# The last feed-forward in sixteen units, with batch 0 carried through the end of the causal attention

## Chip, core and metric

The kernel is one program on one core of a Trainium2 chip. The metric is the device time of one execution in microseconds (us). The time of the kernel before is 565.87 us, the median of three runs from 564.69 to 566.86 us.

## What is computed

The input x holds 2 batches of 256 tokens with 128 features. Four pairs of an attention and a feed-forward are added to it in turn. Only the last feed-forward block matters here; cut to its second half, it is

```
x = x + einsum(attn, wo)                      # causal self-attention, 16 heads of 8
h = x * rsqrt(mean(x*x) + eps) * ln2_w        # per token
p = softmax(h @ gate_w.T)                     # 8 experts
top 2 of p, divided by their sum -> wfull[token, expert], 0 elsewhere
out = 0
for e in range(8):                            # FFN = 256
    g = silu(h @ w1[e].T) * (h @ w3[e].T)
    out = out + (g @ w2[e].T) * wfull[:, e]
x + out
```

All experts are computed for all tokens, in float32, and weighted afterwards.

## The kernel before

The 512 tokens are four tiles of 128 tokens; tiles 0 and 1 are batch 0, tiles 2 and 3 are batch 1. Each engine has one instruction list, written out by hand, and the engines meet only in counting semaphores; `wait_ge(s.name, n)` holds the engine's whole list until the count is there. No planner reorders anything, so the order in the text is the order on the engine.

The causal attention is `attention(2)` on TensorE (PE), ScalarE (ACT) and VectorE (DVE). It runs over 8 groups of 4 heads (`G = 8`); groups 0 to 3 are batch 0, groups 4 to 7 are batch 1. It is a software pipeline of 12 steps: at step s PE does the maxima of group s (`scores_max`), the scores of group s - 2 (`scores_exp`, read by ACT's Exp at L603), probabilities times values of group s - 3 (`probs_values`, L1731 and L1734) and turns the output of group s - 4 (`turn_out`, L1754), after ACT has copied it out (L620); DVE then divides it by its denominators into `Onat` (L944, L947) and counts `o_ready`. From step 8 on no maxima are left: steps 8 to 11 are the drain.

After it come, for all four tiles at once and one behind the other: `project(3)` on PE (turn `Onat` L1840, ACT copy L660, multiply by wo L1844), the addition to x on DVE (L1011), `rms_normalise(10)` (squares on DVE L857, the root on GpSimd (POOL) L481 and L482, the scaling L863), the turn of the normalised rows (L1519), and ACT's copy into `lnT` (L565). Four matrix products without a use, `keep_busy(4, 5)` at L1876, stand on PE between the projection and the turn.

The feed-forward runs over the 8 experts. `up3(e)` multiplies all 512 columns of `lnT` by four 128-wide blocks of w13 (L2178), one PSUM bank for each; ACT takes Silu of the first two banks (L798), DVE multiplies by the other two (L1502). `down3(e)` (L2187) multiplies by w2 into bank 4 or 5, and `add_expert` (L371) adds the four tiles, weighted, to x. On PE the order is up3(e + 1), down3(e). The gate's logits (L2193) follow up3(0); DVE's `route()` (L1479 to L1492, with the helpers at L1021 to L1041) makes the weights, in expert 0, with one Exp on ACT (L801). Each matrix product in float32 stands as two matmul instructions, each with a weight load, in the trace. The output leaves in one store of 256 KB when all eight experts are added (L458).

The first feed-forward of the kernel (L1895, L1907, L1182 and the helpers with a batch argument) is already written in 16 units of one expert and one batch, and it begins in the drain of the first attention.

Of the kernel before, what the change touches and what calls it, by code (L numbers as in the profile page):

```python
# [28 lines left out]
ALU = mybir.AluOpType  # L29
# [58 lines left out]
def mega_kernel(nc, d, out_dram):  # L88

    ctx = ExitStack()  # L90
    with ctx:
# [64 lines left out]
        PT2 = PR[:, 2048:4096].rearrange("p (t k q) -> p t k q", t=NT, k=4)  # L156
        SG = PR[:, 4096:5632].rearrange("p (c t) -> p c t", c=3)
# [115 lines left out]
        NORMS = [(0, 0), (1, 0), (2, 0), (1, 1), (2, 1), (3, 0), (3, 1)] + [(k, 0) for k in range(4, 11)]  # L273
# [90 lines left out]
        def add_expert(dve, e, count, b0, y_base=0):  # L364

            dve.wait_ge(s.y_ready, y_base + e + 1)
            if count:
                dve.wait_ge(s.y_added, count)
            y = bank(b0 + e % 2).rearrange("p (t n) -> p t n", t=NT)
            for t in range(NT):  # L370
                i = dve.scalar_tensor_tensor(out=x[:, t, :], in0=y[:, t, :], scalar=comb[:, t, e:e + 1],  # L371
                                             in1=x[:, t, :], op0=ALU.mult, op1=ALU.add)
            i.then_inc(s.y_added, 1)


        @block.sync
        def _(sp):
# [85 lines left out]
        def _(pool):  # L463
# [90 lines left out]
            rstd_of(10)  # L554
# [3 lines left out]
        def _(act):  # L558
# [24 lines left out]

            def attention(a):
# [220 lines left out]
        def _(dve):  # L805
# [48 lines left out]
            def rms_normalise(k):  # L854

                for t in range(NT):
# [4 lines left out]
                dve.wait_ge(s.rstd_ready, norm(k) + 1)  # L861
                for t in range(NT):
                    i = dve.tensor_scalar(xn[:, t, :], x[:, t, :], rstd[:, t:t + 1], None, ALU.mult)  # L863
                i.then_inc(s.xn_ready, 1)
# [49 lines left out]
            def attention(a):  # L914
# [3 lines left out]
                for step in range(G + 4):  # L918
# [6 lines left out]
                    for part in range(8):  # L925
# [7 lines left out]
                        if a == 0 and step == G + 2 and part == 0:  # L933
                            batch_normalised2(0)
                        g = step - 4
                        if 0 <= g < G:
# [8 lines left out]
                            elif part == 3:  # L945
# [524 lines left out]
            spread_and_stack(dve, ROPE_TILES[4:8], ROPE_TILES)  # L1470
            attention(2)
            project(3, last=False)
            rms_normalise(10)
            dve.wait_ge(s.xn_ready, norm(10) + 1)
            link(dve.tensor_tensor(x_f, x_f, zT, ALU.add))
            def route():

                dve.wait_ge(s.logit_ready, 4)
                link(dve.tensor_copy(lg[:, :, 0:E], bank(6)[:, 0:NT * E].rearrange("p (t e) -> p t e", t=NT)))  # L1479
                link(dve.tensor_reduce(gt[:, :, 0:1], lg[:, :, 0:E], AX_X, ALU.max))  # L1480
                signal(dve.tensor_tensor(lg[:, :, 0:E], lg[:, :, 0:E], gt[:, :, 0:1].to_broadcast([P, NT, E]),
                                       ALU.subtract), 'gate_diff')
                dve.wait_ge(s.gate_exp, 5)
                link(dve.reduce_sum(gt[:, :, 1:2], lg[:, :, 0:E], AX_X))
                link(dve.reciprocal(gt[:, :, 1:2], gt[:, :, 1:2]))
                link(dve.tensor_tensor(lg[:, :, 0:E], lg[:, :, 0:E], gt[:, :, 1:2].to_broadcast([P, NT, E]),
                                       ALU.mult))
                top8(lg)
                one_hots(2)
                link(dve.tensor_tensor(gt[:, :, 0], v8[:, :, 0], v8[:, :, 1], ALU.add))  # L1490
                link(dve.reciprocal(gt[:, :, 0], gt[:, :, 0]))
                link(dve.tensor_tensor(gt[:, :, 1:3], v8[:, :, 0:2], gt[:, :, 0:1].to_broadcast([P, NT, 2]),  # L1492
                                       ALU.mult))
                mix(1, 2)

            for e in range(E):
                for c in range(2):
                    dve.wait_ge(s.act_ready, 4 * NUNIT + 2 * e + c + 1)
                    dve.wait_ge(s.h_ready, 2 * NUNIT + 4 * e + 2 + c + 1)
                    if e >= 2:  # L1500
                        dve.wait_ge(s.y_ready, NUNIT + 2 + e - 1)
                    dve.tensor_tensor(actT[:, e % 2, c, :], SG[:, c, :], bank(2 + c), ALU.mult)\  # L1502
                        .then_inc(s.hd_ready, 1)
                if e == 0:
                    route()
                if e >= 1:
                    add_expert(dve, e - 1, NUNIT + e - 1, 4, NUNIT + 2)
            add_expert(dve, E - 1, NUNIT + E - 1, 4, NUNIT + 2)


        @block.tensor
        def _(pe):
# [245 lines left out]
            def attention(a):  # L1758
                for step in range(G + 4):
                    for part in range(4):  # L1760
                        if step < G:
                            scores_max(a, step, part)
                        if 0 <= step - 2 < G:
                            scores_exp(a, step - 2, part)
                        if part == 0 and 0 <= step - 4 < G:
                            turn_out(a, step - 4)
                        if part == 2 and 0 <= step - 1 < G:
                            turn_max(a, step - 1)
                        if part and 0 <= step - 3 < G:
                            probs_values(a, step - 3, ([], [0], [1], [2, 3])[part])  # L1770

# [398 lines left out]
            def up3(e):  # L2170
                for c in range(4):
                    if e:

                        if c < 2:
                            pe.wait_ge(s.act_ready, 4 * NUNIT + 2 * (e - 1) + c + 1)
                        else:
                            pe.wait_ge(s.hd_ready, NUNIT + 2 * (e - 1) + c - 1)
                    pe.matmul(bank(c), w13[:, e, c * P:(c + 1) * P], lnT[:, :], start=True, stop=True)\  # L2178
                        .then_inc(s.h_ready, 1)

            def down3(e):
                pe.wait_ge(s.hd_ready, NUNIT + 2 * e + 2)
                if e >= 2:
                    pe.wait_ge(s.y_added, NUNIT + e - 1)
                for t in range(NT):
                    for c in range(2):
                        i = pe.matmul(bank(4 + e % 2)[:, t * P:(t + 1) * P], actT[:, e % 2, c, t * P:(t + 1) * P],  # L2187
                                      w2e[:, e, c, :], start=(c == 0), stop=(c == 1))
                i.then_inc(s.y_ready, 1)

            up3(0)
            for t in range(NT):
                i = pe.matmul(bank(6)[:, t * E:(t + 1) * E], lnT[:, t * P:(t + 1) * P], WD["gate3"],  # L2193
                              start=True, stop=True)
            i.then_inc(s.logit_ready, 1)
            for e in range(E):
                if e + 1 < E:
                    up3(e + 1)
                down3(e)
# [100 lines left out]
```

## Time and profile before

| | |
|---|---|
| three runs | 566.86, 564.69, 565.87 us; median 565.87 us |
| the profiled execution | 566.35 us, its span 564.3 us (2.05 us lie outside the span) |
| busy share of the span | PE 89%, DVE 62%, ACT 55%, POOL 11% |
| mean granted TensorE clock | 0.976 |
| chain that ended last, by engine | PE 74%, DVE 11%, ACT 5% |

The span reaches from the first to the last instruction. The chain that ended last is followed back from the last instruction, at each step to what released it. The granted clock is 1.00 at 2.4 GHz and 0.50 at 1.2 GHz.

### The profile page before, as it was taken

What the parts mean: (1) busy time and instruction counts of PE and PEld (TensorE: products, weight loads), DVE (VectorE), ACT (ScalarE), POOL (GpSimd) and SP (SyncE); (2) the same over time, 40 slices, a digit from 0 to 9 for tenths busy, and PEclk for the clock granted to TensorE, in tenths of its full rate; (3) what the DMA queues carried; (4) which work ended last, traced back from release to release, by engine and by line L of the source; (5) the groups of instructions that cost most, each with busy time, mean ns of one, the idle gap of its engine ahead of it and who ended that gap; (6) DMA issues with size and microseconds to landing.
All of it is one profiled execution on the core that took longest, in us unless ns stands there. A gap on an engine that the chain in (4) does not pass through costs nothing.

```text
span 564.3 us, 9091 instructions
## 1 busy us (share of the span) xinstructions
PE 502.2 (89%) x3288; PEld 295.0 (52%) x3288; DVE 351.4 (62%) x905; ACT 311.5 (55%) x534; POOL 62.1 (11%) x159
## 2 busy tenths in 40 slices
PE   6789998999979997798897699999999858878997
PEld 2234456999824444345562345555557455544565
DVE  6757746556888771695246467778871676523644
ACT  7447796463327785256366289878880145553321
POOL 4021120100012110000460000000001310000000
PEclk9979999999989999999998799999999989998999
DMA  4669201034223000000000000000002300000000
GB/s 142 197 193 403 104 2 34 2 98 126 73 78 135 1 1 1 2 0 2 0 0 1 1 0 1 2 0 2 2 1 70 155 1 1 1 2 0 2 1 19
DMA packets 11467, 26.16 MB, mean 46 GB/s; under 512 B 2112, under 2 KB 6592, under 8 KB 10784
## 3 DMA queue, kind: packets, MB, share of 16 engines
q1 hardware_dynamic: 11424, 25.59, 13.7%
q8 instruction: 27, 0.44, 0.3%
q14 instruction: 16, 0.13, 0.1%
HBM read 22.44 MB, written 3.15 MB: 45 GB/s over the span
## 4 chain that ended last, share of the span: by engine, by line
PE 74%; DVE 11%; ACT 5%; issue 4%; SPq 2%; POOL 2%; DMA 1%; DVEq 0%; ACTq 0%; POOLq 0%
PE ps L1790 6%; PE ps L1801 5%; PE ps L1816 5%; PE ps L1907 5%; PE ps L1655 5%; PE ps L1895 5%; PE ps L2178 5%; PE ps L1739 5%; PE ps L1637 4%; DVE mxs L899 3%; PE ps L2187 3%; PE ps L1866 2%; PE ps L2054 2%; PE ps L1876 1%; PE ps L1666 1%
## 5 line engine op out<-in xcount | busy, mean ns | idle before, releaser
L899 DVE TENSOR_REDUCE mxs<-ps 128x1 f32<-128x512 f32 x128 | 81.8, 682 | 25.3 <-PE ps L1655 24.0
L603 ACT ACTIVATE PR<-ps 128x1024 f32<-128x1024 f32 x80 | 77.4, 977 | 35.1 <-PE ps L1637 18.8
L1000 DVE TENSOR_REDUCE nm<-ps 128x1 f32<-128x512 f32 x64 | 41.1, 684 | 25.3 <-PE ps L1790 25.3
L1655 PE MATMUL ps<-Kst,Qst 84*128 84x512 bf16 x128 | 50.1, 399 | 6.9 <-DVE mxs L899 3.8
L644 ACT COPY PR<-ps 128x512 f32<-128x512 f32 x64 | 37.9, 595 | 16.8 <-PE ps L1801 16.8
L652 ACT ACTIVATE Qst<-ps,nm 128x512 f32<-128x512 f32 x64 | 45.4, 709 | 1.5 <-DVE nm L1000 1.3
L1637 PE MATMUL ps<-Qst,Kst 84*128 84x256 bf16 x256 | 46.0, 274 | 0.1
L1801 PEld LDWEIGHTS ps<-const_t,Qst 128*128 128x128 f32 x256 | 27.4, 140 | 24.3 <-DVE Qst L983 11.8
L681 ACT ACTIVATE PR<-ps,cols_t 128x256 f32<-128x256 f32 x64 | 26.6, 471 | 23.4 <-PE ps L1895 23.0
L612 ACT COPY Qst<-ps 12x1024 bf16<-12x1024 bf16 x24 | 24.0, 999 | 26.9 <-PE ps L1712 26.8
L1790 PE MATMUL ps<-VX,FC 64*128 64x512 f32 x128 | 36.1, 641 | 0.1
L1801 PE MATMUL ps<-const_t,Qst 128*128 128x128 f32 x256 | 35.4, 280 | 0.9 <-ACT PR L644 0.9
L1739 PE MATMUL ps<-PR,VX 128*9 128x256 f32 x512 | 33.5, 380 | 0.0
L1876 PE MATMUL ps<-ctxT,const_t 128*128 128x512 f32 x56 | 27.9, 648 | 5.6 <-DMA const_t<-in_const 5.6
L1907 PEld LDWEIGHTS ps<-FC,PR 128*128 128x128 f32 x256 | 30.9, 192 | 0.8
L1895 PE MATMUL ps<-parts,FC 128*128 128x256 f32 x128 | 30.4, 380 | 0.9 <-DVE scr L947 0.8
L1637 PEld LDWEIGHTS ps<-Qst,Kst 84*128 84x128 bf16 x256 | 23.4, 98 | 14.9 <-issue 2.9
L1907 PE MATMUL ps<-FC,PR 128*128 128x128 f32 x256 | 31.0, 275 | 0.0
L1816 PE MATMUL ps<-PR,Kst 128*64 128x256 f32 x256 | 30.9, 385 | 0.0
L1655 PEld LDWEIGHTS ps<-Kst,Qst 84*128 84x128 bf16 x128 | 12.5, 99 | 33.5 <-DVE mxs L899 23.4
L2178 PE MATMUL ps<-scr,FC 128*128 128x512 f32 x64 | 29.0, 595 | 0.8 <-ACT scr L565 0.8
L983 DVE TENSOR_SCALAR Qst<-Qst,rsum 128x512 f32<-128x512 f32 x64 | 28.2, 484 | 1.1
(364 smaller groups left out, 855.9 us busy)
## 6 DMA issues: line engine op xcount, KB each, us to landing
Kst<-k_rows SPq DMA_DIRECT2D x48, 96.0 KB
FC<-in_fc SPq DMA_DIRECT2D x2, 2048.0 KB, 12.2
Qst<-q_rows SPq DMA_DIRECT2D x48, 48.0 KB
FC<-in_w SPq DMA_DIRECT2D x1, 2048.0 KB, 8.4
k_rows<-REP SPq DMA_DIRECT2D x12, 128.0 KB, 2.2
REP<-in_w SPq DMA_DIRECT2D x1, 1536.0 KB, 6.5
q_rows<-REP SPq DMA_DIRECT2D x20, 64.0 KB, 2.0
FC<-in_w2e SPq DMA_DIRECT2D x1, 1024.0 KB, 10.4
```

What stands on the lines that cost most here:

```text
L603: act.activation(PRg[:, g % 2, u * 1024:u * 1024 + width], bank(3 + 2 * (n % 2), 2)[:, 0:width], ACT.Exp, scale=scale).then_inc(s.p_ready, 1)
L652: act.activation(P3[:, i % 8, :], bank(S_BANKS[n % 2][half]), ACT.Exp, bias=nm3[:, i % 8:i % 8 + 1], accum_out=sum3[:, i % 16:i % 16 + 1]) ...
L899: i = dve.tensor_reduce(m[:, u // 4, u % 4:u % 4 + 1], bank(n % 2), AX_X, ALU.max)
L1637: i = pe.matmul(bank(3 + 2 * (n % 2), 2)[:, k * SQ:(k + 1) * SQ], Kst[0:ROWS_A, b, h0 + u, k * P:(k + 1) * P], Qst[0:ROWS_A, b, h0 + u, :] ...
L1655: pe.matmul(bank(n % 2), Qst[0:ROWS_A, b, h, q0:q0 + P], Kst[0:ROWS_A, b, h, :], start=True, stop=True).then_inc(s.smax_ready, 1)
L1739: i = pe.matmul(o[32 * c:32 * c + HD + 1, :], Vaug[:, 4 * b + k, h0 + c, 0:HD + 1], pr[:, c * 1024 + k * SQ:c * 1024 + (k + 1) * SQ], star ...
L1790: pe.matmul(bank(S_BANKS[n % 2][half]), Q3[d0:d0 + DH3, r, q0:q0 + P], K3[d0:d0 + DH3, r, b * SK:(b + 1) * SK], start=True, stop=True)\
L1801: ins = pe.transpose(bank(T_BANKS[half])[:, k * P:(k + 1) * P], P3[:, i % 8, k * P:(k + 1) * P], ident)
L1816: pv = pe.matmul(bank(O_BANKS[g % 2])[DH3 * c:DH3 * (c + 1), r * SQ:(r + 1) * SQ], V3[:, 4 * b + k, DH3 * (h0 + 2 * r + c):DH3 * (h0 + 2 * ...
L1895: i = pe.matmul(bank(2 * (n % 2) + c // 2)[:, c % 2 * SQ:(c % 2 + 1) * SQ], fc1[:, n % E, c * P:(c + 1) * P], hdT[:, n % 3, :], start=True ...
L1907: i = pe.matmul(bank(4 + n % 2)[:, j * P:(j + 1) * P], actT[:, n % 2, c, j * P:(j + 1) * P], fc2[:, n % E, c, :], start=(c == 0), stop=(c ...
L2178: pe.matmul(bank(c), w13[:, e, c * P:(c + 1) * P], lnT[:, :], start=True, stop=True)\
```

## The change

The last feed-forward is cut into 16 units (n = 8 b + e), each one expert for one batch: `unit3_up(n)` has four products of 256 columns, in two banks in place of four; ACT takes Silu of one whole bank, DVE multiplies by the other, `unit3_down(n)` has four products in place of eight, and `add_unit3` adds two tiles. The order on PE is again up(n + 1), down(n).

The projection, the norm, the turns, the logits and the routing become one set for each batch. Batch 0's are put in the drain of the attention: the turn of `Onat` at the start of step 8, the projection at its end, the squares on DVE in step 8, the scaling in step 9, the turn of the rows at the end of step 9, the logits and the first three gate operations in step 10. `unit3_up(0)` stands in step 11 ahead of the last `turn_out`. Batch 1's are put between units 0 and 7. The four idle products of `keep_busy` go. The output leaves in two stores of 128 KB, one for each batch.

```diff
 
-        NORMS = [(0, 0), (1, 0), (2, 0), (1, 1), (2, 1), (3, 0), (3, 1)] + [(k, 0) for k in range(4, 11)]
...
             sp.dma_start(w2e, d["w2e"]).then_inc(s.ld_w2e, 16)
-            sp.wait_ge(s.y_added, NUNIT + E)
-            sp.dma_start(out_dram, x[:, :, :]).then_inc(s.stored, 16)
-            sp.wait_ge(s.stored, 16)
+            for b in range(B):
+                sp.wait_ge(s.y_added, NUNIT + E * (b + 1))
+                sp.dma_start(out_dram[:, of_batch(b), :], x[:, of_batch(b), :]).then_inc(s.stored, 16)
+            sp.wait_ge(s.stored, 16 * B)
...
-            rstd_of(10)
+            for b in range(B):
+                rstd_of(10, b, of_batch(b))
...
+                    if a == 2 and step == G:
+                        onat_rows3_out(0, lnT, bank(0))
+                    if a == 2 and step == G + 2:
+                        rms_out(0, bank(0))
...
             attention(2)
-            onat_out(2)
-            ln_out(10)
-            for e in range(E):
-                for c in range(2):
-                    act.wait_ge(s.h_ready, 2 * NUNIT + 4 * e + c + 1)
-                    if 2 * e + c >= 2:
-                        act.wait_ge(s.hd_ready, NUNIT + 2 * e + c - 1)
-                    act.activation(SG[:, c, :], bank(c), ACT.Silu).then_inc(s.act_ready, 1)
-                if e == 0:
-                    act.wait_ge(s.gate_diff, 5)
-                    act.activation(lg[:, :, 0:E], lg[:, :, 0:E], ACT.Exp).then_inc(s.gate_exp, 1)
+            gate_exp3(0)
+            for n in range(NUNIT):
+                act.wait_ge(s.h_ready, 2 * NUNIT + 2 * n + 1)
+                if n >= 2:
+                    act.wait_ge(s.hd_ready, NUNIT + n - 1)
+                act.activation(SG[:, n % 2, :], bank(2 * (n % 2)), ACT.Silu).then_inc(s.act_ready, 1)
+                if n == 1:
+                    onat_rows3_out(1, OT, bank(7))
+                if n == 4:
+                    rms_out(1, bank(7))
+                if n == 6:
+                    gate_exp3(1)
...
+            def rms_projected(b, at):
+
+                dve.wait_ge(s.proj_ready, 5 + b + 1)
+                link(dve.tensor_tensor(x[:, of_batch(b), :], x[:, of_batch(b), :],
+                                       at[:, 0:SQ].rearrange("p (t n) -> p t n", t=2), ALU.add))
+                for t in (2 * b, 2 * b + 1):
                     i = dve.tensor_tensor_reduce(out=rest[:, t * P:(t + 1) * P], in0=x[:, t, :],
                                                  in1=x[:, t, :], scale=1.0 / P, scalar=0.0, op0=ALU.mult,
                                                  op1=ALU.add, accum_out=mv[:, t, 1:2])
                 i.then_inc(s.var_ready, 1)
...
+            def rms_normalised(b):
+
+                dve.wait_ge(s.rstd_ready, norm(10, b) + 1)
+                for t in (2 * b, 2 * b + 1):
                     i = dve.tensor_scalar(xn[:, t, :], x[:, t, :], rstd[:, t:t + 1], None, ALU.mult)
-                i.then_inc(s.xn_ready, 1)
+                signal_xn(i, norm(10, b) + 1)
+                link(dve.tensor_tensor(x[:, of_batch(b), :], x[:, of_batch(b), :],
+                                       zT[:, b * SQ:(b + 1) * SQ].rearrange("p (t n) -> p t n", t=2), ALU.add))
+
+            def signal_xn(ins, count):
+
+                ins.then_inc(s.xn_ready, 1)
+                dve.wait_ge(s.xn_ready, count)
...
                             batch_normalised2(0)
+                        if a == 2 and step == G + 1 and part == 1:
+                            rms_normalised(0)
...
+                                if a == 2 and step == G:
+                                    rms_projected(0, bank(1))
+                                if a == 2 and step == G + 2:
+                                    route_logits(0)
...
+            for n in range(NUNIT):
+                dve.wait_ge(s.act_ready, 4 * NUNIT + n + 1)
+                dve.wait_ge(s.h_ready, 2 * NUNIT + 2 * n + 2)
+                if n >= 2:
+                    dve.wait_ge(s.y_ready, NUNIT + 2 + n - 1)
+                dve.tensor_tensor(acts3[:, n % 2, :, :].rearrange("p c t -> p (c t)"), SG[:, n % 2, :],
+                                  bank(2 * (n % 2) + 1), ALU.mult).then_inc(s.hd_ready, 1)
+                if n == 0:
+                    route(0)
+                if n >= 1:
+                    add_unit3(n - 1)
+                if n == 2:
+                    rms_projected(1, bank(6)[:, SQ:2 * SQ])
+                if n == 3:
+                    rms_normalised(1)
+                if n == 5:
+                    route_logits(1)
+                if n == 7:
+                    route(1)
+            add_unit3(NUNIT - 1)
...
+                        if step == G and part == 0:
+                            pe.wait_ge(s.smax_read, MAXB[a + 1])
+                            turn_onat3(0, bank(0))
...
                         if part == 0 and 0 <= step - 4 < G:
+                            if step == G + 3:
+                                pe.wait_ge(s.ld_w13, 16)
+                                pe.wait_ge(s.ld_w2e, 16)
+                                unit3_up(0)
...
+                        if step == G + 2 and part == 2:
+                            logits3(0)
...
+                    if step == G:
+                        project_rows3(0, lnT, bank(1))
+                    if step == G + 1:
+                        turn_rows(10, 0, bank(0))
...
+            def unit3_up(n):
+
+                b, e = divmod(n, E)
+                pe.wait_ge(s.lnT_ready, TURNS.index((10, b)))
+                for c in range(4):
+                    if n >= 2 and c == 0:
+                        pe.wait_ge(s.act_ready, 4 * NUNIT + n - 1)
+                    if n >= 2 and c == 2:
+                        pe.wait_ge(s.hd_ready, NUNIT + n - 1)
+                    i = pe.matmul(bank(2 * (n % 2) + c // 2)[:, c % 2 * SQ:(c % 2 + 1) * SQ],
+                                  w13[:, e, c * P:(c + 1) * P], lnT[:, b * SQ:(b + 1) * SQ], start=True, stop=True)
+                    if c % 2:
+                        i.then_inc(s.h_ready, 1)
...
+            def unit3_down(n):
+
+                pe.wait_ge(s.hd_ready, NUNIT + n + 1)
+                if n >= 2:
+                    pe.wait_ge(s.y_added, NUNIT + n - 1)
+                for j in range(2):
+                    for c in range(2):
+                        i = pe.matmul(bank(4 + n % 2)[:, j * P:(j + 1) * P], acts3[:, n % 2, c, j * P:(j + 1) * P],
+                                      w2e[:, n % E, c, :], start=(c == 0), stop=(c == 1))
+                i.then_inc(s.y_ready, 1)
 
...
             pe.wait_ge(s.masks_ready, 3)
             pe.wait_ge(s.ld_onesel, 16)
-            attention(2)
-            project(3, 2, WD["wo3f"])
-            keep_busy(4, 5)
-            turn_xn(10)
-            pe.wait_ge(s.lnT_ready, 11)
-            pe.wait_ge(s.ld_w13, 16)
-            pe.wait_ge(s.ld_w2e, 16)
...
-            for e in range(E):
-                if e + 1 < E:
-                    up3(e + 1)
-                down3(e)
+            attention_self(2)
+            for n in range(NUNIT):
+                if n == 0:
+                    pe.wait_ge(s.o_ready, 3 * G)
+                if n + 1 < NUNIT:
+                    unit3_up(n + 1)
+                unit3_down(n)
+                if n == 0:
+                    turn_onat3(1, bank(7))
+                if n == 1:
+                    pe.wait_ge(s.gate_diff, 5)
+                    project_rows3(1, OT, bank(6)[:, SQ:2 * SQ])
+                if n == 3:
+                    turn_rows(10, 1, bank(7))
+                if n == 4:
+                    logits3(1)
```

The new functions on PE, cut from the diff above: `turn_onat3` turns two tiles of `Onat`, `project_rows3` multiplies two tiles by wo (four matmul instructions), `logits3` multiplies two tiles by the gate's weights. On ACT `onat_rows3_out` and `rms_out` copy 256 columns, and `gate_exp3` is one Exp of 2 x 8 values. On DVE `route_logits` is the first three operations of the old `route()`, `route` the rest of it, both over two tiles.

## Rows read from the trace of the kernel before

**Rows 1.** Chain that ended last, in order of time: start us, us, what.

```profile
508.69 0.23 DVE scr L947
...
510.30 1.75 PE ps L1844 x8
512.04 4.52 PE ps L1876 x8
...
517.78 3.70 PE ps L2178 x8
521.48 0.79 PE ps L2193 x8
...
527.59 3.44 PE ps L2178 x8
531.03 1.78 PE ps L2187 x16
...
557.13 3.58 PE ps L2187 x32
```

**Rows 2.** Timeline, the end: start us, us, engine line operation count [idle before].

```profile
560.74 1.12 DVE L371 SCALAR_TENSOR_TENSOR x<-ps,comb,x 128x128 f32<-128x128 f32 x4 [0.66 <-PE ps L2187]
561.89 0.34 SPq L458 DMA_DIRECT2D out<-x  x1
```

**Rows 3.** Windows: length, busy PE, PEld, DVE, ACT, POOL, granted clock, DMA share, GB/s.

```profile
500.00:510.00 10.00, 6.69 (x71) 3.40 (x70) 1.29 (x6) 4.91 (x9) 0.00 (x0) 1.00 0.01 2
510.00:520.00 10.00, 8.92 (x25) 4.87 (x26) 3.19 (x14) 3.01 (x5) 1.27 (x2) 0.83 0.00 0
```

**Rows 4.** Timeline of PE in the drain of the causal attention.

```profile
502.46 0.41 PE L1754 MATMUL ps<-const_t,scr 128*128 128x128 f32 x2 [1.29 <-ACT scr L620]
...
506.25 0.44 PE L1754 MATMUL ps<-const_t,scr 128*128 128x128 f32 x2 [0.59 <-ACT scr L620]
...
507.08 0.40 PE L1734 MATMUL ps<-PR,FC 128*32 128x128 f32 x8
```

**Rows 5.** Timeline of PE in the first feed-forward's units.

```profile
89.00 1.96 PE L1895 MATMUL ps<-parts,FC 128*128 128x256 f32 x8
...
92.00 1.97 PE L1895 MATMUL ps<-parts,FC 128*128 128x256 f32 x8 [0.82 <-DVE scr L947]
...
95.59 0.38 PE L1533 MATMUL ps<-const_t,scr 128*128 128x128 f32 x2
95.81 1.89 PE L1895 MATMUL ps<-parts,FC 128*128 128x256 f32 x8
97.54 1.95 PE L1907 MATMUL ps<-FC,PR 128*128 128x128 f32 x16
99.32 0.61 PE L1540 MATMUL ps<-wa_t,scr 128*128 128x128 f32 x4
99.77 1.89 PE L1895 MATMUL ps<-parts,FC 128*128 128x256 f32 x8
```

**Rows 6.** Timeline of POOL, ACT and DVE around the norm and the gate.

```profile
514.14 1.04 POOL L482 TENSOR_TENSOR rstd<-ve,nhalf 128x4 f32<-128x4 f32 x1
...
523.23 1.28 ACT L798 ACT_TABLE_LOAD   x1
523.31 0.19 DVE L1484 TENSOR_REDUCE gt<-lg 128x4 f32<-128x32 f32 x1 [0.36 <-ACT lg L801]
...
526.55 0.19 DVE L1041 TENSOR_TENSOR comb<-oh 128x32 f32<-128x32 f32 x1
```

**Rows 7.** Groups by line of DVE and ACT: busy us, mean ns, idle before.

```profile
L1502 DVE TENSOR_TENSOR PR<-PR,ps 128x512 f32<-128x512 f32 x16 | 10.9, 686 | 13.9 <-ACT PR L798 8.7 <-PE ps L2178 5.0
...
L1182 DVE SCALAR_TENSOR_TENSOR x<-ps,comb,x 128x128 f32<-128x128 f32 x32 | 9.7, 346 | 17.9 <-PE ps L1907 17.8
...
L798 ACT ACTIVATE PR<-ps 128x512 f32<-128x512 f32 x16 | 9.4, 597 | 23.5 <-PE ps L2178 23.4
```

**Rows 8.** Groups by line and form, weight loads of the first feed-forward.

```profile
L1895 PEld LDWEIGHTS ps<-parts,FC 128*128 128x128 f32 x128 | 23.2, 190 | 5.1 <-issue 2.6
```

More of the change, by code:

```diff
@@ L271, in mega_kernel @@
         NUNIT = B * E
-        NORMS = [(0, 0), (1, 0), (2, 0), (1, 1), (2, 1), (3, 0), (3, 1)] + [(k, 0) for k in range(4, 11)]
+        NORMS = [(0, 0), (1, 0), (2, 0), (1, 1), (2, 1), (3, 0), (3, 1)] + [(k, 0) for k in range(4, 10)] + [(10, 0), (10, 1)]
         def norm(k, b=0):
@@ L362, in group_heads @@
             return g // 4, 4 * (g % 4)
[L364 to L373, printed above, removed]
         @block.sync
@@ L582, in gate_exp0, with onat_rows3_out, rms_out, gate_exp3 @@
                 act.activation(gt[:, of_batch(b), 1], gt[:, of_batch(b), 0], ACT.Exp).then_inc(s.gate_exp, 1)
+            def onat_rows3_out(b, to, at):
+                act.wait_ge(s.onat_turned, 3 + b + 1)
+                act.copy(to[:, 0:SQ], at[:, 0:SQ]).then_inc(s.onatT_ready, 1)
+            def rms_out(b, at):
+                act.wait_ge(s.xn_turned, TURNS.index((10, b)) + 1)
+                act.activation(lnT[:, b * SQ:(b + 1) * SQ], at[:, 0:SQ], ACT.Copy, scale=CB["rms2"])\
+                    .then_inc(s.lnT_ready, 1)
+            def gate_exp3(b):
+                act.wait_ge(s.gate_diff, 5 + b)
+                act.activation(lg[:, of_batch(b), 0:E], lg[:, of_batch(b), 0:E], ACT.Exp).then_inc(s.gate_exp, 1)
             def attention(a):
@@ L1470, in _ @@
             spread_and_stack(dve, ROPE_TILES[4:8], ROPE_TILES)
-            attention(2)
[L1472 to L1494, printed above, removed]
@@ L1496, in _ @@
-            for e in range(E):
[L1497 to L1507, printed above, removed]
@@ new lines, in route @@
+            def route(b):
+                at = of_batch(b)
+                dve.wait_ge(s.gate_exp, 5 + b)
+                link(dve.reduce_sum(gt[:, at, 1:2], lg[:, at, 0:E], AX_X))
+                link(dve.reciprocal(gt[:, at, 1:2], gt[:, at, 1:2]))
+                link(dve.tensor_tensor(lg[:, at, 0:E], lg[:, at, 0:E], gt[:, at, 1:2].to_broadcast([P, 2, E]),
+                                       ALU.mult))
+                top8(lg, 2 * b, 2 * b + 2)
+                one_hots(2, 2 * b, 2 * b + 2)
+                link(dve.tensor_tensor(gt[:, at, 0], v8[:, at, 0], v8[:, at, 1], ALU.add))
+                link(dve.reciprocal(gt[:, at, 0], gt[:, at, 0]))
+                link(dve.tensor_tensor(gt[:, at, 1:3], v8[:, at, 0:2], gt[:, at, 0:1].to_broadcast([P, 2, 2]),
+                                       ALU.mult))
+                mix(1, 2, 2 * b, 2 * b + 2)
@@ new lines, in add_unit3 @@
+            def add_unit3(n):
+                b, e = divmod(n, E)
+                dve.wait_ge(s.y_ready, NUNIT + 2 + n + 1)
+                dve.wait_ge(s.y_added, NUNIT + n)
+                y = bank(4 + n % 2)[:, 0:SQ].rearrange("p (t n) -> p t n", t=2)
+                for j in range(2):
+                    t = 2 * b + j
+                    i = dve.scalar_tensor_tensor(out=x[:, t, :], in0=y[:, j, :], scalar=comb[:, t, e:e + 1],
+                                                 in1=x[:, t, :], op0=ALU.mult, op1=ALU.add)
+                i.then_inc(s.y_added, 1)
@@ L1768, in attention, with turn_onat3 @@
                             turn_max(a, step - 1)
+                        if step == G + 2 and part == 2:
+                            logits3(0)
                         if part and 0 <= step - 3 < G:
                             probs_values(a, step - 3, ([], [0], [1], [2, 3])[part])
+                    if step == G:
+                        project_rows3(0, lnT, bank(1))
+                    if step == G + 1:
+                        turn_rows(10, 0, bank(0))
+            def turn_onat3(b, to):
+                pe.wait_ge(s.o_ready, 2 * G + G // 2 * (b + 1))
+                for j in range(2):
+                    i = pe.transpose(to[:, j * P:(j + 1) * P], Onat[:, 2 * b + j, :], ident)
+                i.then_inc(s.onat_turned, 1)
@@ new lines, in project_rows3, with logits3 @@
+            def project_rows3(b, turned, to):
+                pe.wait_ge(s.onatT_ready, 3 + b + 1)
+                for j in range(2):
+                    i = pe.matmul(to[:, j * P:(j + 1) * P], turned[:, j * P:(j + 1) * P], WD["wo3f"],
+                                  start=True, stop=True)
+                i.then_inc(s.proj_ready, 1)
+            def logits3(b):
+                pe.wait_ge(s.lnT_ready, TURNS.index((10, b)))
+                for t in (2 * b, 2 * b + 1):
+                    i = pe.matmul(bank(6)[:, t * E:(t + 1) * E], lnT[:, t * P:(t + 1) * P], WD["gate3"],
+                                  start=True, stop=True)
+                i.then_inc(s.logit_ready, 1)
```

43 lines of the change are left out of this document (13 added, 30 removed).

## Prediction, made before the changed kernel was run

> **What bounds the kernel now.** I read the chain that ended last first, from its end backwards. The reader is to see that from 517.78 us on it is PE alone: up3 takes 3.44 us, down3 1.78 us, 5.22 us for an expert, and the last down3 ends at 560.7 us [rows 1]. So in the feed-forward only PE's own work sets the end. Before it stands a bridge: from the last division on DVE (508.69 + 0.23 = 508.92 us) to the first up3 at 517.78 us the chain passes through the projection, the norm, the turn and their copies, 8.86 us, in which PE does little that is needed [rows 1]. Then I read the timeline of PE in the drain, for what idles there: PE waits 1.29 us before one `turn_out` and 0.59 us before the next, both times for ACT's copy [rows 4]; in 500 to 510 us it is busy 6.69 us of 10 and DVE 1.29 us [rows 3]. Last I read the first feed-forward, which has the form that the new one will have; its pitches are the prices below [rows 5].
>
> **The feed-forward itself costs PE the same.** There, eight matmuls of 256 columns take 97.54 - 95.81 = 1.73 us, and sixteen of 128 columns 99.32 - 97.54 = 1.78 us [rows 5]. A new unit has eight of the first kind and eight of the second: 1.73 + 0.89 = 2.62 us. Two units are 5.24 us, against 5.22 us for an expert before [rows 1].
>
> **Batch 0's set in the drain** is costed at nothing up to the logits, and this is what hides it. The turn of `Onat` (0.22 us on PE, 95.59 to 95.81 [rows 5]) needs groups 0 to 3, long divided by step 8, and falls before `turn_out` of group 4, which waits for ACT. The projection (four matmuls, 99.77 - 99.32 = 0.45 us [rows 5]) falls into the idle 1.29 us; the turn of the rows (0.22 us) into the 0.59 us [rows 4]. Without this cover the three cost 0.89 us. On DVE, `rms_normalised(0)` adds a wait for POOL's root (1.04 us [rows 6]); behind it in DVE's list stands the division of group 5, and behind that `turn_out` of group 6 at 506.25 us [rows 4]. The chain from the projection's end (501.7 us: the wait ends at 502.46 and begins 1.29 before, plus 0.45) is an addition over 256 columns (between 0.35 and 0.69 us, half and whole of the 512-column operation [rows 7]; I take 0.4), squares, root and scaling, some 2.7 us with the waits: rows scaled by about 504.8 us, group 5 divided by about 505.8 us. That is 0.45 us before it would be late, a slim cover.
>
> The logits are not covered: four matmuls, half of the 0.79 us that eight took [rows 1], 0.4 us, ahead of the last probabilities times values, which ended at 507.08 + 0.40 = 507.48 us [rows 4]. So `unit3_up(0)` starts at about 507.9 us.
>
> **The joint.** Up(0) goes ahead of the last `turn_out`, so the last division comes up to 1.73 us later, and up(1) waits for it (`o_ready`). The first feed-forward had the same order: its up(0) began at 89.00 us and its up(1) at 92.00 us, with 0.82 us of idle PE before it [rows 5]. I take these 3.0 us: up(1) at 510.9 us. Behind up(1)'s wait stands everything else on PE. The Silu table's load (1.28 us [rows 6]) begins on ACT before the data is there, and ends by about 509.9 us; Silu 0 and product 0 are done by 511.4 us, before down(0) at 512.6 us.
>
> **From up(1) to the end on PE:** 15 x 1.73 = 25.95; 16 x 0.89 = 14.24; batch 1's two turns 0.44, projection 0.45, logits 0.4. Sum 41.5 us.
>
> **Waits inside.** In a free unit, product n is ready 0.15 + 0.69 us after up(n) ends [rows 7], and down(n) comes only after down(n - 1) and up(n + 1), 2.62 us after: 1.8 us of slack. The gate eats it twice. After product 0, `route(0)` holds DVE; the old one took 526.55 + 0.19 - 523.31 = 3.43 us for four tiles [rows 6]. For two tiles it lies between half of that and all; nearly all its operations are small, so I take 3.0. Then product 1 is ready 0.4 us before down(1). For batch 1, ACT does load, Exp, load (1.28 + 0.21 + 1.28 = 2.8 us [rows 6]) after Silu 6, and Silu 7 queues behind. Counted from the start of up(7): Silu 6 ends at -1.0, the loads at 1.8, Silu 7 (0.60 [rows 7]) at 2.4, product 7 at 3.1, the addition of unit 6 at 3.75, `route(1)` at 6.75, product 8 at 7.45; down(8) is due at 3 x 1.73 + 2 x 0.89 = 6.97. PE waits 0.5 us; with a route of 3.43 it is 0.9, with half of it nothing. Batch 1's norm is done by unit 5 and first needed in up(8). ACT, with one Silu of 0.60 us per 2.62, has room else.
>
> **The end.** Before, 560.74 to 561.89 us for four additions, then the store, to 564.3 us [rows 2]. Now two additions, 0.6 us by 2 x 346 ns less their overlap [rows 7]. The last store has half the bytes; a smaller one is between half of 2.41 us and no gain, and I take no gain. The first store's 128 KB go out during batch 1's units; SP's list holds nothing else that anyone waits for. The matmuls' result comes 0.17 us after their pitch ends (1.95 against 1.78 [rows 5]).
>
> **The sum:** 507.9 + 3.0 + 41.5 + 0.5 + 0.17 + 0.04 + 0.6 + 0.03 + 2.41 = 556.15 us for the span, against 564.3: 8.15 us less. The profiled execution was 566.35 us, so 558.2 us for it; it stood 0.48 us above the median of the runs shown, so I predict a median of 557.7 us. The likeliest case's own range is 556.5 to 559.3: down by the 0.5 us of the wait and 0.7 of the store, up by the 0.89 us in the drain and 0.7 for longer routes.
>
> **Rivals.** *The clock halves once.* In 510 to 520 us before, the granted clock was 0.83 on average, after 10 us with PE busy 6.69 us [rows 3]; at the levels 2.4 and 1.2 GHz that is 3.4 us at the lower one, 1.7 us of lost work. Now PE has some 2.9 us more to do in the drain, which speaks against it, but the joint leaves it idle 0.8 us. Time 559.4, chance 0.17.
>
> *The gate costs more than the slack*, at both places by a microsecond: 559.7, chance 0.1. It takes routes longer than the old one, or a late division of group 5.
>
> *It does not do what it says.* DVE becomes the bound, so that the bridge comes back in pieces: about 565.5, no change, chance 0.03. It needs 0.5 us more for each of 16 units, thus a pitch above 3.1 us; DVE's product and additions are 1.3 us.
>
> *Slower: the weight loads come out.* 16 units have 256 weight loads, 8 experts had 192. The 64 more at 0.19 us each [rows 8], if nothing hid them, are 12.2 us: 569.9. It decides when more than 8.15 / 64 = 0.13 us of each shows. Against it: at 256 columns a matmul and its load keep a pitch of 1.73 / 8 = 0.216 us, half of the 0.43 us of 512 columns [rows 1, 5]. Chance 0.04. The Trainium skill, Perfetto Trace Analysis, section Matmuls, speaks for this rival: "Larger matmuls are more efficient than smaller matmuls, when possible." By that rule the halved products would cost time; by the rows of the first feed-forward they cost 0.02 us per expert.
>
> **How the numbers follow.** The forecast has the remaining 0.66. About 0.5%, 2.8 us, is what a measurement of this kernel can tell from no change. Faster: 0.66 + 0.17 + 0.1 = 0.93; within: 0.03; slower: 0.04. The range takes in the own range and the two rivals just above it: 556.3 to 561.0.
>
> **What would show it.** In the changed trace: up(0) within 0.3 us of 507.9 and up(1) 3.0 us later, or the drain or the joint is mispriced; a pitch of 2.62 us between units with PE at 9 to 10 tenths, or the weight loads show; a wait of PE of 0.5 us before down(8) put down to DVE, and nowhere else over 0.2 us; clock 1.00 from 500 us on; the last additions 0.6 us. The prediction is wrong if PE idles more than 2 us in all after up(1), or if group 5's division holds PE in the drain.

## The result and the profile after

The changed kernel took 558.49 us (median of four runs, 558.11 to 559.39), the one before 566.37 us (four, 564.69 to 567.83). The ratio is 0.9864, with the interval 0.984 to 0.9888: faster by 1.4%. The forecast was 557.7 us in a range of 556.3 to 561.0. The profiled execution took 559.39 us, its span 557.4 us, where 558.2 and 556.15 had been worked out.

The spans differ by only 6.9 us, where 8.15 was forecast. The difference is therefore read from a landmark, the turn at the start of step 8 of the causal attention (`turn_out` of group 4). In the timelines of PE, before and after, it is

```profile
497.88 0.41 PE L1754 MATMUL ps<-const_t,scr 128*128 128x128 f32 x2 [0.64 <-issue]
```

```profile
498.43 0.44 PE L1841 MATMUL ps<-const_t,scr 128*128 128x128 f32 x2
499.14 0.41 PE L1806 MATMUL ps<-const_t,scr 128*128 128x128 f32 x2 [0.27 <-issue]
```

From its start to the end of the span there are 66.42 us before and 58.26 us after, 8.16 us less (forecast: 556.15 - 497.88 = 58.27). One piece of the change stands ahead of it, the turn of batch 0's `Onat` (L1841). It lies in idle time of PE and moves the landmark by nothing: from the start of the last probabilities times values ahead of it to the landmark there are 1.06 us in both kernels (496.82 to 497.88, 498.08 to 499.14). The 1.26 us by which the landmark itself is later came in further ahead, in code that the change does not touch, where the granted clock was lower in this execution. The view is that of windows (stretch, then busy time of PE, PEld, DVE, ACT and POOL, the granted clock, the DMA share and GB/s); first the kernel after:

```profile
450.00:460.00 10.00, 6.28 (x69) 6.16 (x70) 7.61 (x26) 4.90 (x9) 2.16 (x4) 0.72 0.01 2
460.00:470.00 10.00, 8.05 (x62) 5.62 (x61) 6.54 (x17) 2.36 (x3) 0.00 (x0) 0.67 0.00 0
470.00:480.00 10.00, 9.22 (x90) 5.66 (x92) 5.73 (x16) 5.54 (x8) 0.00 (x0) 0.93 0.01 2
...
500.00:510.00 10.00, 9.12 (x92) 5.11 (x91) 3.29 (x16) 5.64 (x10) 0.95 (x2) 1.00 0.01 2
510.00:520.00 10.00, 9.37 (x56) 8.31 (x55) 6.77 (x32) 4.04 (x6) 0.39 (x2) 1.00 0.00 1
```

and the same early stretches of the kernel before:

```profile
450.00:460.00 10.00, 5.02 (x61) 4.91 (x62) 8.05 (x28) 4.84 (x12) 3.38 (x7) 0.83 0.00 0
460.00:470.00 10.00, 7.05 (x80) 4.89 (x78) 7.30 (x18) 3.93 (x6) 0.00 (x0) 1.00 0.01 2
470.00:480.00 10.00, 8.87 (x93) 5.31 (x93) 5.90 (x17) 6.14 (x9) 0.00 (x0) 1.00 0.01 2
```

The two later stretches of after answer to [rows 3]: PE is busy 9.12 and 9.37 us of 10, at clock 1.00 in both. All comparisons below are made from the landmark to the end of the span.

The chain that ended last, from the last division on, answers to [rows 1]:

```profile
511.92 0.23 DVE scr L974
...
512.20 1.99 PE ps L1869 x8
...
535.67 0.19 DVE comb L1072
535.88 0.70 DVE PR L1546
536.62 1.16 PE ps L1881 x8
...
552.61 2.01 PE ps L1881 x16
554.64 0.35 DVE x L1536
```

Before, 8.86 us lay between the last division and the first up product. Now it is 0.05 us (511.92 + 0.23 to 512.20): up(1), batch 0's second unit, goes at once. From the landmark, up3(0) stood at 19.90 us, up(1) stands at 13.06 us; that is 6.84 of the 8.16 us. The rest of PE's work takes 42.44 us instead of 42.96 (512.20 to 554.64, and 517.78 to 560.74), and the end 2.76 us instead of 3.56: 0.52 and 0.80 us, which complete the 8.16.

The timeline of PE, from the landmark on, answers to [rows 4]:

```profile
502.37 0.71 PE L1848 MATMUL ps<-wd_t,scr 128*128 128x128 f32 x4
503.73 0.41 PE L1806 MATMUL ps<-const_t,scr 128*128 128x128 f32 x2 [0.65 <-ACT scr L631]
...
506.86 0.44 PE L1578 MATMUL ps<-const_t,xn 128*128 128x128 f32 x2
507.52 0.44 PE L1806 MATMUL ps<-const_t,scr 128*128 128x128 f32 x2 [0.23 <-ACT scr L631]
...
508.46 0.61 PE L1856 MATMUL ps<-wd_t,scr 128*128 128x8 f32 x4
...
509.36 1.99 PE L1869 MATMUL ps<-scr,FC 128*128 128x256 f32 x8
511.19 0.38 PE L1806 MATMUL ps<-const_t,scr 128*128 128x128 f32 x2
512.20 1.99 PE L1869 MATMUL ps<-scr,FC 128*128 128x256 f32 x8 [0.63 <-DVE scr L974]
```

The idle 1.29 and 0.59 us of before are 0.65 and 0.23 us: the projection (L1848) and the turn of batch 0's rows (L1578) stand in them. Up(0) fills most of the time in which the last group is turned and divided.

Last the timelines of DVE, POOL and the store's queue, which answer to [rows 6] (root, route) and [rows 2] (end):

```profile
504.48 0.72 POOL L472 TENSOR_TENSOR rstd<-ve,nhalf 128x2 f32<-128x2 f32 x1
...
506.46 0.22 DVE L974 TENSOR_TENSOR scr<-ps,rden 128x64 f32<-128x64 f32 x1
...
552.71 0.69 DVE L1546 TENSOR_TENSOR PR<-PR,ps 128x512 f32<-128x512 f32 x1 [1.18 <-ACT PR L807]
...
554.64 0.61 DVE L1536 SCALAR_TENSOR_TENSOR x<-ps,comb,x 128x128 f32<-128x128 f32 x2 [0.50 <-PE ps L1881]
555.28 0.34 SPq L448 DMA_DIRECT2D out<-x  x1
```

Of the executions timed for the table below, one of the kernel with batch 0's set behind the attention took 1685.03 us and is left out of its ratio.

### The profile page after: what moved, and what is told of

Same layout as the page of the kernel before. It is cut to its first block, busy times and chain, and to the rows that moved or that the text cites. A ratio compares the mean times of both kernels' runs of the same rounds, so it can differ in the third digit from the quotient of the medians.

```text
span 557.4 us, 9259 instructions
## 1 busy us (share of the span) xinstructions
PE 503.7 (90%) x3340; PEld 308.6 (55%) x3344; DVE 354.4 (64%) x922; ACT 312.1 (56%) x537; POOL 62.5 (11%) x161
## 4 chain that ended last, share of the span: by engine, by line
PE 75%; DVE 10%; ACT 5%; issue 4%; DMA 2%; SPq 2%; POOL 1%; DVEq 0%; ACTq 0%; POOLq 0%
PE ps L1903 6%; PE ps L1914 6%; PE ps L1929 5%; PE ps L2020 5%; PE ps L2008 5%; PE ps L1707 5%; PE ps L1791 5%; PE ps L1869 4%; PE ps L1689 4%; DVE mxs L924 3%; PE ps L1979 2%; PE ps L1881 2%; PE ps L2167 2%; PE ps L1989 2%; PE ps L1718 1%
## 5 line engine op out<-in xcount | busy, mean ns | idle before, releaser
L1869 PE MATMUL ps<-scr,FC 128*128 128x256 f32 x128 | 30.6, 382 | 0.6 <-DVE scr L974 0.6
L1989 PE MATMUL ps<-ctxT,const_t 128*128 128x512 f32 x48 | 23.6, 640 | 5.7 <-DMA const_t<-in_const 5.7
```

Source lines behind the costliest of these rows:

```text
L1869: i = pe.matmul(bank(2 * (n % 2) + c // 2)[:, c % 2 * SQ:(c % 2 + 1) * SQ], w13[:, e, c * P:(c + 1) * P], lnT[:, b * SQ:(b + 1) * SQ], sta ...
```

## The experiments

Each was timed beside the kernel before on the same chip. "To the end" is the time from the landmark to the end of the span in the profiled execution.

| kernel | time, us | ratio to before | to the end, us |
|---|---|---|---|
| before | 566.37 | | 66.42 |
| changed | 558.49 | 0.984 to 0.9888 | 58.26 |
| changed, again | 558.13 | 0.9822 to 0.9891 | 58.25 |
| before, cut into units alone | 567.51 | 1.0008 to 1.0046 | 67.39 |
| before, PE kept busy in the drain | 566.6 | 0.9975 to 1.0013 | 65.68 |
| changed, batch 0's set behind the attention | 567.53 | 0.9999 to 1.0041 | 67.16 |
| the same, PE kept busy | 565.5 | 0.9963 to 1.0001 | 65.25 |
| changed, batch 1's set between units 7 and 8 | 566.57 | 0.9965 to 1.0006 | 65.65 |
| changed, up(0) in two halves | 556.94 | 0.9794 to 0.986 | 57.67 |
| changed, up(0) behind the last turn | 558.8 | 0.981 to 0.9881 | 58.03 |
| changed, one store | 559.97 (one run) | | 58.56 |
| halves, and the second route a unit later | 557.25 | 0.9797 to 0.986 | 57.29 |

The theory is that the bridge of 8.86 us between attention and feed-forward has been filled, half of it in the drain (batch 0) and half among batch 0's units (batch 1). Its rivals: the cut into units is the gain, or the clock is.

**The changed kernel again**, a control.

> The changed kernel once more, as the measure for the other runs beside it on the same chip: 558.5 us, between 558 and 559.5.

The time to the end was 58.25 us against 58.26 in the first profile, equal within the 0.1 us to which a span is given, while the start of step 8 had moved from 499.14 to 497.15 us. So differences of some tenths in this measure can be read from single profiles, though not from the times.

**The cut alone.** The kernel before with the units of the change; bridge, gate, idle products and the single store stay.

```diff
...
-            for e in range(E):
-                if e + 1 < E:
-                    up3(e + 1)
-                down3(e)
+            for n in range(NUNIT):
+                if n + 1 < NUNIT:
+                    unit3_up(n + 1)
+                unit3_down(n)
```

> The kernel before with its feed-forward cut into sixteen units and nothing else moved: the bridge, its four idle products, one gate for all tiles and one store stay. By my theory PE pays 0.02 us per expert for the cut (0.16 us), the last additions give back 0.5 us, and the gate over four tiles (3.43 us on DVE) now makes PE wait once, about 0.9 us, before down(1): 566.4 + 0.6 = 567.0 us, between 565.8 and 567.8. By the rival that the 64 more weight loads come out at 0.19 us each it is 12 us longer, 578. If the cut itself were the gain, it would be near 558.5.

It took 0.97 us longer to the end. The pitch, from the start of one unit's products to the start of the next, is 2.62 us (526.45 to 529.07 in PE's timeline), so the weight loads stay hidden. What is added is a wait at the gate:

```profile
522.75 1.89 PE L2189 MATMUL ps<-scr,FC 128*128 128x256 f32 x8
525.45 1.16 PE L2201 MATMUL ps<-FC,PR 128*128 128x128 f32 x8 [0.81 <-DVE PR L1513]
526.45 1.89 PE L2189 MATMUL ps<-scr,FC 128*128 128x256 f32 x8
...
529.07 1.89 PE L2189 MATMUL ps<-scr,FC 128*128 128x256 f32 x8
```

Up(2) is through at 522.75 + 1.73 = 524.48 us, and down(1) starts at 525.45: 0.97 us lost, and 0.11 more because down(1) takes 1.00 us instead of 0.89. With eight times 0.02 us of pitch and some 0.2 us at the last unit, PE needs 1.45 us more from the first up product to the last additions (517.41 to 561.82, 44.41 us, against 42.96). The end gives back 0.48 us (3.08 instead of 3.56), about what was expected of two additions in place of four; 0.97 us are left. The cut by itself is no gain. The Trainium skill (Perfetto Trace Analysis, section Matmuls) prefers larger matmuls where they are possible; for halving 512 columns to 256 the trace bears that out only by those 0.02 us per expert.

**The clock alone.** The kernel before, with products without a use put into the drain; nothing reads them.

```diff
+                    if step == G:
+                        pe.wait_ge(s.smax_read, MAXB[a + 1])
+                    for _ in range((5, 2, 2, 2)[step - G] if step >= G else 0):
+                        pe.matmul(bank(1), identb[:, :], onesel[:, :, :], start=True, stop=True)
```

> The kernel before with eleven products without a use (bf16, 512 columns, 0.22 us each) put into PE's idle time in the drain: five at the end of step 8, two at the end of steps 9, 10 and 11. If they keep the granted clock at 1.00 through 510 to 520 us, the projection takes 0.9 us in place of 1.75. By my theory the clock was worth no more than that in the old bridge, plus some 0.2 us of the idle products' overrun: 565.3 us, and 566.4 if the clock falls all the same. By the rival that the change won its time by keeping the clock up, most of the 7.9 us would show here: 562 or less.

To the end it was 0.74 us shorter, and the time did not change measurably. The window says that the clock did stay up, against 0.83 in [rows 3]:

```profile
510.00:520.00 10.00, 7.88 (x27) 4.00 (x27) 3.19 (x14) 3.69 (x5) 1.27 (x2) 1.00 0.01 2
```

The clock is therefore worth 0.74 us of the 8.16 where the bridge stands; it is not the cause. Nor are the four idle products, which stand on the chain of [rows 1] with 4.52 us: at the full clock they are done early here, PE waits 0.67 us behind them for DVE's scaling (the turn starts at 516.01 us), and still only 0.74 us are gained.

**Batch 0's set out of the drain.** The changed kernel, with batch 0's turn, projection, norm, logits and up(0) behind the attention, and batch 1's set where the change has it.

```diff
...
-                            if step == G + 3:
-                                pe.wait_ge(s.ld_w13, 16)
-                                pe.wait_ge(s.ld_w2e, 16)
-                                unit3_up(0)
...
+                    turn_onat3(0, bank(0))
+                    project_rows3(0, lnT, bank(1))
+                    turn_rows(10, 0, bank(0))
+                    logits3(0)
...
+                    unit3_up(0)
```

> The changed kernel with batch 0's set taken out of the drain: turn, projection, norm, turn, logits and up(0) come after the attention's last division, one behind the other; batch 1's set stays between the units, and there are no idle products. By my theory the drain is where most of the gain lies: the chain for two tiles is about 5.2 us, logits 0.4 and up(0) 1.73 behind it, so up(1) starts 7.3 us after the last division in place of about 1.9 us: 5.4 us longer than the changed kernel, 563.9 us, up to 565 if the clock halves. By the rival that it is the split by batch that hides the bridge, wherever batch 0's set stands, it stays within 1 us of 558.5.

It gave back 8.9 us, more than the whole gain and more than expected. PE's timeline and a window:

```profile
513.25 0.69 PE L1573 MATMUL ps<-const_t,xn 128*128 128x128 f32 x2 [2.71 <-DVE xn L879]
514.50 1.02 PE L1838 MATMUL ps<-wd_t,scr 128*128 128x8 f32 x4 [0.56 <-ACT scr L583]
515.37 6.39 PE L1851 MATMUL ps<-scr,FC 128*128 128x256 f32 x16
```

```profile
510.00:520.00 10.00, 6.73 (x21) 5.25 (x22) 3.10 (x13) 2.57 (x4) 0.96 (x2) 0.53 0.00 1
```

The bridge is back with its 2.71 us of idle PE, and at the lower clock the up products of the first two units take 6.2 us (515.37 to 521.60) instead of 3.46. The clock did not fall behind that idle time, but at its front: PE falls idle at 510.54 us, and in windows of 1 us (length, busy time of PE alone, granted clock, DMA share, GB/s) the clock goes down in that same microsecond:

```profile
509.00:510.00 1.00, 0.54 (x3) 1.00 0.00 0
510.00:511.00 1.00, 0.54 (x4) 0.79 0.00 0
511.00:512.00 1.00, 0.00 (x0) 0.50 0.00 0
```

It does so in the kernel before as well (0.85 in 510 to 511 us, 0.50 in the next), where PE is at work on the projection by then. What both have ahead of it is the drain. To part the chain of waits from the clock, **the same with products without a use** in the drain and, as the kernel before had, behind it:

```diff
...
+                    for _ in range((5, 2, 2, 2)[step - G] if step >= G else 0):
+                        pe.matmul(bank(1), identb[:, :], onesel[:, :, :], start=True, stop=True)
...
+                    keep_busy(3, 5)
```

> The kernel of the run without the drain (batch 0's set behind the attention's last division), with products without a use put in for the clock alone: the eleven small ones of the run with the busy drain, and three of 0.86 us between batch 0's projection and its turn. The time is read from the start of step 8's turn of group 4 to the end of the span: 58.26 us in the changed kernel, 67.16 without the drain. If of these 8.9 us 5.4 are the chain of waits and 3.4 the clock, which was at half from 510.8 to 520.6 us, this one takes 63.5 to 64.2 us, with a granted clock of 1.00 throughout. If the chain alone is the price and the clock only went along with it, it stays at 67.

The clock was 1.00 from 510 to 520 us, and 1.9 us came back of the 8.9: 65.25 us, about one more than expected. PE's timeline shows the rest of the miss:

```profile
515.12 3.70 PE L1855 MATMUL ps<-scr,FC 128*128 128x256 f32 x16
519.32 1.16 PE L1867 MATMUL ps<-FC,PR 128*128 128x128 f32 x8 [0.50 <-DVE PR L1541]
...
520.53 1.89 PE L1855 MATMUL ps<-scr,FC 128*128 128x256 f32 x8
522.83 1.16 PE L1867 MATMUL ps<-FC,PR 128*128 128x128 f32 x8 [0.40 <-DVE PR L1541]
```

At full clock PE reaches down(0) and down(1) before DVE has products 0 and 1: 0.74 us between the pitch end of up(1) and down(0), 0.57 us between up(2) and down(1). At half clock PE came late enough not to wait. So without the drain up(1) starts 5.5 us later (515.12 + 1.73, 18.6 us from the landmark, against 13.06), some 1.4 us are lost around the gate, and 1.9 us to the clock.

**Batch 1's set in one piece** between units 7 and 8, instead of spread over units 0 to 7.

```diff
...
-                if n + 1 < NUNIT:
+                if n + 1 < NUNIT and n != 7:
...
-                if n == 0:
+                if n == 7:
...
```

> The changed kernel with batch 0 in the drain as it is, but batch 1's set not spread over units 0 to 7: turn, projection, norm, turn, logits stand between down(7) and up(8), its routing behind product 8. By my theory the spread hides a second chain of the same length: PE waits 4.9 us more between down(7) and up(8), and the 0.3 us before down(8) go: 62.9 to 63.4 us from step 8's turn of group 4 to the end, against 58.26. If the clock falls in that gap as it did without the drain, up to 66. If the batches' independence is worth little by itself, because DVE and ACT have room to catch up, it stays below 60.

It gave back 7.4 us. PE's timeline and the windows:

```profile
537.55 0.44 PE L1574 MATMUL ps<-const_t,xn 128*128 128x128 f32 x2 [2.69 <-DVE xn L879]
538.55 1.02 PE L1852 MATMUL ps<-wd_t,scr 128*128 128x8 f32 x4 [0.56 <-ACT scr L583]
539.43 6.29 PE L1865 MATMUL ps<-scr,FC 128*128 128x256 f32 x16
```

```profile
530.00:540.00 10.00, 6.19 (x37) 5.17 (x36) 3.75 (x15) 2.73 (x4) 0.95 (x2) 0.89 0.00 0
540.00:550.00 10.00, 10.00 (x44) 8.45 (x43) 6.26 (x29) 3.29 (x5) 0.00 (x0) 0.77 0.05 15
```

The bridge for one batch idles PE for 2.69 us at one place alone, and the clock falls: the up products of units 8 and 9 take 6.13 us to 545.56 instead of 3.46, 2.7 us more. Without these, 4.7 us are left for the waits, where 4.6 were expected (4.9 less 0.3); that split is read from the trace, and no run with the clock kept up was made here. Both halves of the change are needed: with either one undone, and the clock falling as it did, the time is that of before. With the clock kept up and batch 0's set behind the attention, 65.25 us to the end, 1.2 of the 8.16 us are left.

**The joint.** Two kernels shift up(0) against the last `turn_out`: in halves around it, and wholly behind it.

```diff
-                                unit3_up(0)
+                                unit3_up(0, (0, 1))
...
+                            if step == G + 3:
+                                unit3_up(0, (2, 3))
...
```

> The changed kernel with up(0) split around the last turn of the attention's output: its first two blocks ahead of it, its last two behind it. By my theory the joint's idle time on PE (0.63 us before up(1), and some 0.2 before it) is the price of putting all 1.73 us of up(0) ahead: the last division comes 0.87 us earlier, and up(1) starts 2.0 to 2.2 us after up(0) in place of 2.84: 0.6 to 0.85 us shorter than the changed kernel. If something else released up(1) (ACT's table load, the gate), it stays the same.

```diff
+                            turn_out(a, step - 4)
+                            if step == G + 3:
                                 unit3_up(0)
-                            turn_out(a, step - 4)
```

> The changed kernel with all of up(0) behind the last turn of the attention's output. By my theory PE then idles 0.5 us for ACT's copy ahead of the turn, and nothing after up(0): up(1) starts about 2.45 us after the time at which up(0) could have started, against 2.84: 0.4 us shorter than the changed kernel. By the rival that up(0) must stand ahead to cover the wait for the division, it is 0.5 us or more longer.

In halves, the division runs while PE does the second half, and up(1) follows without a gap, 2.06 us after the start of up(0) instead of 2.84. Of these 0.78 us 0.59 reach the end, just short of the 0.6 expected: down(1) now waits for product 1, which ends behind the gate at 514.30 us, and starts at 514.35. PE's timeline shows twelve matmuls in a row, the last four of up(0) and up(1):

```profile
508.72 2.78 PE L1871 MATMUL ps<-scr,FC 128*128 128x256 f32 x12
```

Wholly behind, the idle 0.63 us in front of up(1) goes too, but 0.65 us of idle PE appear ahead of the last turn, and 0.23 us are left of an expected 0.4.

**One store** for both batches.

```diff
-            for b in range(B):
-                sp.wait_ge(s.y_added, NUNIT + E * (b + 1))
-                sp.dma_start(out_dram[:, of_batch(b), :], x[:, of_batch(b), :]).then_inc(s.stored, 16)
...
+            sp.wait_ge(s.y_added, NUNIT + NUNIT)
+            sp.dma_start(out_dram, x[:, :, :]).then_inc(s.stored, 16)
...
```

> The changed kernel with one store of 256 KB at the end in place of two of 128 KB. The time from the end of the last addition to the end of the span was 2.41 us before and 2.15 us in the changed kernel. By my theory the half store is what made it shorter: 2.4 us here. If the order of the stores or their number costs or gains something else, it stays at 2.15 or goes past 2.6.

DVE's last additions, at 554.93 us:

```profile
554.93 0.61 DVE L1535 SCALAR_TENSOR_TENSOR x<-ps,comb,x 128x128 f32<-128x128 f32 x2 [0.49 <-PE ps L1880]
```

They end at 555.54 us, the span at 558.0: 2.46 us, against 2.15 us with two stores (555.25 to 557.4). By the same two points it was 2.44 us before (561.86 to 564.3); the 2.41 us of the expectation are counted from the start of the store, 561.89. This run is a single profile, but the others say the same: the four profiles with one store have 2.44 to 2.47 us, the eight with two stores 2.12 to 2.19. The split is worth 0.3 us.

**The best version.** Up(0) in halves, and `route(1)` on DVE moved from unit 7 to behind the product of unit 8.

```diff
+                if n == 8:
+                    route(1)
...
-                if n == 7:
-                    route(1)
...
```

> The split of up(0), and batch 1's routing on DVE moved from unit 7 to unit 8, behind that unit's product. In the changed kernel PE waits 0.30 us before down(8), for product 8 behind the routing; that wait should go, and down(9) then has 0.1 us of slack by the same count. Together 0.9 to 1.15 us shorter than the changed kernel, 557.4 us. If the wait only moves from down(8) to down(9), it equals the split alone.

To the end 57.29 us, 0.97 us less than the changed kernel and the least of all. The wait before down(8) is gone: up(9) and up(10) stand one pitch apart, where the changed kernel had 3.03 us (534.59 to 537.62).

```profile
532.36 1.89 PE L1871 MATMUL ps<-scr,FC 128*128 128x256 f32 x8
534.98 1.89 PE L1871 MATMUL ps<-scr,FC 128*128 128x256 f32 x8
```

Its time, 557.25 us, beats the kernel before, and its profile that of the changed one; in the times it cannot be told from the halves alone.

## Why the prediction was right

**Mechanism.** It held: the bridge ceased to be on the chain that ended last. Batch 0's half put back costs 8.9 us, 1.9 of them through the clock, and batch 1's 7.4, of which 2.7 go with the clock by the reading above. The two do not add up to the 8.16 us of the gain, since with either one undone a whole chain of waits stands on PE again. The cut alone costs time, and the clock in the old bridge (0.74 us) and the store (0.3 us) explain tenths.

**Drain.** Up(0) was forecast 10.02 us from the landmark and came at 10.22; most of the 0.20 is the logits, which took 0.54 us (508.46 to 509.00) of 0.4. Group 5 was divided at 506.68 us, and the turn behind it on PE started at 507.52: 0.84 us of slack, where 0.45 had been worked out. POOL's root took 0.72 us for two columns instead of the 1.04 that four took. What fell short was the sentence "Without this cover the three cost 0.89 us": that is PE's share alone. Out of the drain the set costs 8.9 us, because its copies, norm and waits on ACT, DVE and POOL come back with it, and the clock falls (1.9 us).

**Joint.** 2.84 us between up(0) and up(1), of 3.0; idle PE 0.63 us, where the first feed-forward had 0.82.

**PE from up(1) to its last result.** Pitch 2.62 us, as priced, at clock 1.00: the rivals of the weight loads, the gate and the halved clock did not come. The whole took 42.42 us against 42.17 (41.5 + 0.5 + 0.17). The wait before down(8) was 0.30 us instead of 0.5, mostly since `route(1)` took 2.86 us (532.99 to 535.85) in place of 3.0 and began 0.1 us sooner (load, Exp, load ahead of it took the 2.8 us forecast, though the Exp is 0.23 us and not 0.21 in the trace of before); PE's products took 0.29 us more at three places, up(1) at 1.83, up(6) at 1.81 and down(8) at 1.00 us instead of 1.73, 1.73 and 0.89. One wait had been overlooked: the 1.8 us of slack is that of a unit which another follows. Behind up(15) there is no up(16), so down(15) is due at 552.45 + 0.89 = 553.34 us, and product 15 ends at 553.40. That this is most of the remaining delay, some 0.2 us, is worked out from the records, not tried.

**End.** Additions 0.61 us, of 0.6. The store had been priced at no gain and gained 0.3: from its start to the end of the span 2.12 us (555.28 to 557.4) instead of 2.41.

**Sum.** The late up(0) (+0.20) and the extra PE time (+0.25) are balanced by the joint (-0.16) and the store (-0.29). That 58.26 stands against 58.27 is therefore chance; the terms themselves were off by up to 0.3 us each. What stands between 557.7 us and the two measured medians of 558.49 and 558.13 is no larger than the variation of the landmark from run to run (497.15 to 499.14 us for this one kernel).

## What to carry to other kernels

A serial stretch between two dense stages can be taken off the path when the work divides into independent parts: one part's copy of it goes into the idle places of the stage before, the other's among the first part's units, and here neither half was enough alone. Price such a stretch by its whole chain, not by the busy time it takes on the bounding engine, and look at the last unit by itself, which has no successor to hide its wait. For tenths of a microsecond measure from a landmark in the trace just ahead of the change: the times contain what the clock did elsewhere.

## What the runs showed of the hardware

The granted clock fell after stretches in which PE had idled, but not only behind a long gap. In the kernel before, and again with batch 0's set out of the drain, it went from 1.00 to 0.50 within 510 to 511 us, after a drain (500 to 510 us) in which PE was busy 6.69 and 6.61 us of 10 with no gap above 1.3 us; with PE kept busy in that drain it stayed at 1.00. With batch 1's set in one piece it fell at about 538 us, behind a gap of 2.69 us. The up products of two units at the lower clock took 2.7 to 2.8 us more. The clock also fell in unchanged code between 450 and 480 us in one execution (0.72, 0.67, 0.93), and less in another of the same kernel (0.83, 1.00, 1.00). A lower clock can cost less than the engine's own work shows, when PE would have waited anyway: with batch 0's set out of the drain, keeping it up returned 1.9 us, less than the 2.8 us of those up products alone, because PE then waited for DVE at the gate. A store of half the bytes ended the span 0.3 us sooner, and POOL's root took 0.72 us for 128x2 and 1.04 for 128x4.
